# Segment sums moved from the end to the middle of a step, and one block further behind, in a graph network layer

## What is computed

```python
msg_in = jnp.concatenate([node_features[row], node_features[col]], axis=-1)
h = jax.nn.relu(msg_in @ Wm1 + bm1)
h = jax.nn.relu(h @ Wm2 + bm2)
messages = h @ Wm3 + bm3
agg = jax.ops.segment_sum(messages, col, num_segments=num_nodes)
agg = agg / jnp.clip(count, 1.0)[:, None]
```

## Time and profile before

| what | us |
|---|---|
| median of three runs | 1428.48 |
| lowest and highest | 1424.92 and 1430.98 |
| the profiled execution | 1430.17 |
| its span, first to last instruction | 1428.2 |
| PE busy in the span | 1289.8 (90%) |
| DVE busy | 994.0 (70%) |
| ACT busy | 732.5 (51%) |
| POOL busy | 760.7 (53%) |

### The profile page before, as it was taken

The page is one execution under the profiler, slowest core; times in us unless marked ns, Lnnn a source line. Parts: engine busy times, 40 slices in busy tenths (PEclk is TensorE's granted clock), DMA queues, the critical chain, the costliest instruction groups (busy, mean ns, idle before and its releaser), DMA issues.

```text
span 1428.2 us, 32880 instructions
## 1 busy us (share of the span) xinstructions
PE 1289.8 (90%) x9777; PEld 1184.9 (83%) x9778; DVE 994.0 (70%) x2126; ACT 732.5 (51%) x1323; POOL 760.7 (53%) x806
## 2 busy tenths in 40 slices
PE   5887999999999999999999999999888888987997
PEld 4766999999999898998988888888888888884564
DVE  4334777777777777777777777777777777774555
ACT  2433666565655555555555555555555554542322
POOL 4007777666666666666666666666556565610000
PEclk8767999999999999999999999999999999999999
DMA  6866666555555555555555544555455444410001
GB/s 166 287 228 187 180 177 176 167 170 160 172 157 159 161 163 153 156 157 156 153 153 156 150 148 144 152 150 151 137 149 145 141 150 133 150 53 1 20 26 46
DMA packets 152019, 208.50 MB, mean 146 GB/s; under 512 B 23801, under 2 KB 120553, under 8 KB 151978
## 3 DMA queue, kind: packets, MB, share of 16 engines
q1 hardware_dynamic: 113502, 104.44, 24.7%
q0 software_dynamic: 37632, 102.81, 24.1%
q10 hardware_dynamic: 844, 0.79, 0.3%
HBM read 185.15 MB, written 22.80 MB: 146 GB/s over the span
## 4 chain that ended last, share of the span: by engine, by line
PE 74%; DVE 10%; issue 8%; DVEq 3%; ACT 2%; DMA 2%; ACTq 1%; SPq 0%; POOL 0%
PE bank L932 30%; PE bank L911 11%; PE bank L892 8%; PE bank L894 6%; PE bank L879 6%; DVE onehot L670 3%; DVE agg L684 3%; PE bank L845 3%; ACT h L487 2%; PE bank L980 2%; PE bank L993 2%; PE bank L981 1%; PE bank L969 1%; DVE bank L702 1%; PE bank L957 1%
## 5 line engine op out<-in xcount | busy, mean ns | idle before, releaser
L420 POOL DMA_INDIRECT a_edge<-a_table,src_idx x784 | 743.7, 949 | 487.2 <-PE bank L911 263.5
L932 PE MATMUL bank<-w,h 128*128 128x256 f32 x4704 | 622.0, 281 | 0.0
L932 PEld LDWEIGHTS bank<-w,h 128*128 128x128 f32 x4704 | 586.1, 189 | 0.0
L487 ACT ACTIVATE h<-bank 128x512 fp32r<-128x512 f32 x392 | 234.8, 599 | 401.3 <-PE bank L879 401.3
L737 DVE SCALAR_TENSOR_TENSOR h_lo<-bank,h_hi 128x512 fp32r<-128x512 f32 x392 | 270.2, 689 | 126.1 <-ACT h_hi L494 123.0
L725 DVE SCALAR_TENSOR_TENSOR h<-bank,h 128x512 fp32r<-128x512 f32 x392 | 270.7, 691 | 74.2 <-ACT h L487 58.9
L892 PE MATMUL bank<-h_hi,onehot 128*128 128x258 f32 x880 | 237.7, 294 | 66.4 <-DVE onehot L670 66.1
L494 ACT ACTIVATE h_hi<-bank 128x512 fp32r<-128x512 f32 x392 | 235.1, 600 | 120.4 <-PE bank L932 120.0
L911 PE MATMUL bank<-ident,a_edge 128*128 128x128 f32 x1568 | 239.8, 275 | 26.2 <-issue 21.6
L670 DVE SCALAR_TENSOR_TENSOR onehot<-iota,first_node,dst_col 128x256 fp32r<-128x256 int16 x440 | 210.3, 478 | 65.7 <-issue 40.1
L892 PEld LDWEIGHTS bank<-h_hi,onehot 128*128 128x128 f32 x880 | 166.4, 189 | 86.4 <-issue 57.2
(11 more groups left out here) (108 smaller groups left out, 569.5 us busy)
## 6 DMA issues: line engine op xcount, KB each, us to landing
b_win<-b_table SPq DMA_DIRECT2D x392, 128.0 KB
rel<-rel_dram SPq DMA_DIRECT2D x196, 128.0 KB, 3.2
a_edge<-a_table,src_idx POOLq DMA_INDIRECT x784
b_table<-work SPq DMA_DIRECT2D x12, 1024.0 KB, 4.8
a_table<-work SPq DMA_DIRECT2D x12, 512.0 KB, 3.2
f_x<-in_x SPq DMA_DIRECT2D x12, 256.0 KB, 5.4
out<-work SPq DMA_DIRECT2D x12, 256.0 KB, 2.3
work<-in_L_gnn_Wm ACTq DMA_DIRECT2D x2, 256.0 KB, 6.0
```

The source lines that it names most:

```text
L420: pool.indirect_dma_start(a_edge[:, b % R * TB + t, :], None, a_table, bass.IndirectOffsetOnAxis(ap=src_idx[:, b * TB + t:b * TB + t + 1], ...
L487: act.activation(h1[:, k % 2, 0, :], bank[k % 2][:, :], ACT.Relu).then_inc(s_h1h, 1)
L932: ins = pe.matmul(to, h1[:, j, a, h * EB + t * P:h * EB + (t + 1) * P], w2[:, b, h, :], start=False, stop=(a == 1 and h == KH - 1), skip_g ...
```

## The change

On PE the segment sums move: in step k, S(k-3) now stands behind E(k) and ahead of W(k-1), where it was S(k-2) behind W(k-1). At a border S'(k-3) comes behind S(k-3) and no longer ahead of it. The last pass has one more step.

On DVE a step is now OT(k+1), D2(k-2), D1(k), F(k-3), O(k-2), O'(k-2). D2 is done one step later than before, and ahead of D1; F comes behind D1, and ahead of O. Inside F the bank `SUM` is added first, then `SUM_MORE`; an addition no longer waits for the one ahead of it, and the zeroing waits for the addition from `SUM` alone. The test for far one-hots (line 665) moves from ahead of O to behind it. The words for PE and DVE are laid out for the new distance, with one more bit (2^20) for O' of the next step; that is two more small DVE instructions in the setup. ACT, POOL and SP are as before.

```diff
         def steps(i):
-            return range(U + 2) if isinstance(i, int) and i == NI - 1 else range(U)
+            return range(U + 3) if isinstance(i, int) and i == NI - 1 else range(U)
...
             def add_sums(b, w):
-                dve.wait_ge(s_add, added)
                 dve.reg_add(added, added, 1)
...
-                with dve.If(word > 2**14 - 1):
+                with dve.If((word & 64) > 0):
+                    dve.wait_ge(s_sg, i * U + (k + 1))
+                    add_sums(SUM, within(w, 0, NW - 1))
+                dve.reg_mov(summed, added)
+                further = (word >> 14) & 63
+                with dve.If(further > 0):
                     dve.wait_ge(s_sgm, more)
                     add_sums(SUM_MORE, within(w + 1, 1, NW - 1))
...
                 with dve.If((word & 64) > 0):
-                    dve.wait_ge(s_sg, i * U + (k + 1))
-                    add_sums(SUM, within(w, 0, NW - 1))
-                    dve.wait_ge(s_add, added)
+                    dve.wait_ge(s_add, summed)
                     dve.memset(bank[SUM][:, 0:HC], 0.0).then_inc(s_add, 1)
...
+                    if there(i, k) and there(i, k + 1):
+                        if (k + 1) % 2 == 0:
+                            dve.wait_ge(s_rc[(k + 1) // 2 % RC], (i + (k + 1) // U) * 16 + 16)
+                        make_onehot_t(k + 1)
                     if there(i, k - 2):
-                        make_onehot(k % 2, i, k - 2, 0, s_oh)
+                        dve.wait_ge(s_h2h, i * U + (k - 1))
+                        dve.scalar_tensor_tensor(h2_lo[:, k % 2, :, :],
...
+                    if there(i, k - 3):
+                        with dve.If((word & (64 + 63 * 2**14)) > 0):
+                            finish_sums(i, k - 3, word)
                     if there(i, k - 2):
-                        with dve.If(word > 2**14 - 1):
+                        make_onehot(k % 2, i, k - 2, 0, s_oh)
+                        with dve.If(word > 2**20 - 1):
                             make_further_onehot(i, k - 2, 1)
...
+                    if there(i, k - 3):
+                        pe.wait_ge(s_h2l, i * U + (k - 2))
+                        pe.wait_ge(s_oh, i * U + (k - 2))
+                        sum_segments(bank[SUM], (k - 3) % 2, k - 3, False).then_inc(s_sg, 1)
+                        with pe.If(word > 127):
+                            with pe.Fori(1, within(word >> 7, 1, NW - 1) + 1):
+                                sum_further(k - 3)
                     if there(i, k - 1):
                         j = (k - 1) % 2
...
-                    if there(i, k - 2):
-                        pe.wait_ge(s_h2l, i * U + (k - 1))
-                        pe.wait_ge(s_oh, i * U + (k - 1))
-                        with pe.If(word > 127):
-                            with pe.Fori(1, within(word >> 7, 1, NW - 1) + 1):
-                                sum_further(k - 2)
-                        sum_segments(bank[SUM], k % 2, k - 2, False).then_inc(s_sg, 1)
```

More of the change, by code:

```diff
@@ L281, in gnn_layer @@
         PE_TOP = NFE + 128 * (NW - 1)
-        DVE_TOP = (NW - 1) + 64 + 128 * NFE + 2**14 * (NW - 1)
+        DVE_TOP = (NW - 1) + 64 + 128 * NFE + 2**14 * (NW - 1) + 2**20
         full = E // EB
@@ L604, in make_words @@
                 dve.tensor_tensor(words_pe[0:1, 0:NB], words_pe[0:1, 0:NB], far, ALU.add).then_inc(s_wz, 1)
-                dve.scalar_tensor_tensor(words_dve[0:1, 2:2 + NB], row_more[0:1, :], float(2**14),
+                dve.scalar_tensor_tensor(words_dve[0:1, 3:3 + NB], row_more[0:1, :], float(2**14),
+                                         words_dve[0:1, 3:3 + NB], ALU.mult, ALU.add).then_inc(s_wz, 1)
+                dve.tensor_scalar(row_flush[0:1, :], row_more[0:1, :], 1.0, None, ALU.min).then_inc(s_wz, 1)
+                dve.wait_ge(s_wz, 7)
+                dve.scalar_tensor_tensor(words_dve[0:1, 2:2 + NB], row_flush[0:1, :], float(2**20),
                                          words_dve[0:1, 2:2 + NB], ALU.mult, ALU.add).then_inc(s_wz, 1)
-                dve.wait_ge(s_wz, 6)
+                dve.wait_ge(s_wz, 8)
                 dve.scalar_tensor_tensor(words_dve[0:1, 0:NB], row_far[0:1, 1:1 + NB], 128.0,
@@ L646, in _ @@
             added = dve.alloc_register("sums_added_dve")
+            summed = dve.alloc_register("sum_bank_read_dve")
+            dve.reg_mov(summed, 0)
             dve.reg_mov(far_t, 1)
@@ L663, in far_onehots_t @@
             def far_onehots_t(k, word):
-                spans = (word >> 7) & 127
-                with dve.If(spans > 0):
-                    with dve.Fori(1, within(spans, 1, NFE) + 1) as j:
-                        make_far_onehot_t(k, j)
+                with dve.Fori(1, within((word >> 7) & 127, 1, NFE) + 1) as j:
+                    make_far_onehot_t(k, j)
             def make_onehot(slot, i, k, w, done):
@@ L688, in finish_sums @@
                 w = word & 63
-                with dve.If(word > 2**14 - 1):
+                with dve.If((word & 64) > 0):
[4 more added lines that the diff above has]
+                with dve.If(further > 0):
                     dve.wait_ge(s_sgm, more)
                     add_sums(SUM_MORE, within(w + 1, 1, NW - 1))
-                    with dve.If(word > 2**15 - 1):
-                        with dve.Fori(2, within(word >> 14, 2, NW - 1) + 1) as j:
+                    with dve.If(further > 1):
+                        with dve.Fori(2, within(further, 2, NW - 1) + 1) as j:
                             dve.wait_ge(s_add, added)
@@ L727, in body @@
                                                  ).then_inc(s_h1l, 1)
+                    if there(i, k - 3):
+                        with dve.If((word & (64 + 63 * 2**14)) > 0):
+                            finish_sums(i, k - 3, word)
                     if there(i, k - 2):
-                        with dve.If(word > 2**14 - 1):
+                        make_onehot(k % 2, i, k - 2, 0, s_oh)
+                        with dve.If(word > 2**20 - 1):
                             make_further_onehot(i, k - 2, 1)
                     if there(i, k) and there(i, k + 1):
-                        if (k + 1) % 2 == 0:
-                            dve.wait_ge(s_rc[(k + 1) // 2 % RC], (i + (k + 1) // U) * 16 + 16)
-                        make_onehot_t(k + 1)
-                    if there(i, k - 1):
-                        dve.wait_ge(s_h2h, i * U + k)
-                        dve.scalar_tensor_tensor(h2_lo[:, (k - 1) % 2, :, :],
-                                                 bank[2 + (k - 1) % 2][:, :].rearrange("p (t h) -> p t h", t=TB),
-                                                 0.0, h2_hi[:, (k - 1) % 2, :, 0:H].bitcast(F32),
-                                                 ALU.max, ALU.subtract).then_inc(s_h2l, 1)
-                    with dve.If(word > 63):
-                        if there(i, k - 2):
-                            finish_sums(i, k - 2, word)
-                        if there(i, k) and there(i, k + 1):
+                        with dve.If((word & (127 * 2**7)) > 0):
                             far_onehots_t(k + 1, word)
```

7 lines of the change are left out of this document (5 added, 2 removed).

## The result

The changed kernel takes 1598.35 us (median of 4 runs, 1593.16 to 1602.48) where the kernel before takes 1426.7 (4 runs): the ratio is 1.120, 95% interval 1.115 to 1.125. It is 12% slower, where 2% faster was forecast. Four runs of a later group (before_pad4, after_lean_align, before_align, after_compactb) come from a time in which every kernel took some 13% longer, the kernel before too (1619 us), so their times are compared with that one only.

A forecast was written before the change was run, and what follows sets the result against it. PE was taken to set the time, so only its holes could be won. 1430.2 - 46.6 (borders) + 11.5 (passes' ends) + 3 + 2 = 1400.1 us for the profiled execution, 1399 for the median, range 1368 to 1424.

The forecast's parts named there:

- What bounds the kernel: PE sets the time, busy 1009 of 1100 us; only its holes at borders (108 us) and passes' ends (43 us) can be won.
- Plain blocks: Blocks away from borders and passes' ends stay at 2.57 us from W to W, priced at zero change.
- The border: Where windows meet: one wait of 0.70 us remains, cost 1.29 in place of 2.26, gain 46.6 us over 48 borders.
- The upper end of the wait: At a border, S's wait for O with the upper ends of DVE's chain: 1.32 us where 0.70 was taken.
- the lowest gain: All 48 borders with the upper ends of DVE's chain: 48 x 0.35 = 17 us.
- The pass's end: PE's own hole goes, but S waits behind ACT's load: 1.14 us in place of 0.90, a loss of 11.5 us.
- the sum: Whole kernel: 1430.2 - 46.6 + 11.5 + 3 + 2 = 1400.1 us for the profiled execution, taken as 1399 for the median.
- rival 4: DVE's start of a pass gets slow by fetching longer code: decides from 2.2 us, 1438 at 3 us; chance 0.03.
- the slack of O: At a pass's start, the some 1.6 us that DVE was said to have in hand.
- Rival 1: At borders DVE's additions don't get shorter, register work not having been hidden: 1425 to 1432 us, no change; chance 0.11.
- Rival 2: At passes' ends ACT's load does not bind and the hole goes altogether: 1343 us; chance 0.07.
- Rival 3: In every block DVE's chain D2, D1, tests, O outlasts PE's block: slower, 1459 us at 0.15 beyond; chance 0.04.

The follow-up runs named there:

- before_pad4: Kernel before with four waits per block added in never-run code of DVE's loop (430 instructions): 1621 us where the kernel before took 1619.
- after_lean_align: The lean form with ACT's words moved seven places, so its load starts at a multiple of eight: ratio 0.973 to the kernel before at 1619.25 us.
- before_align: Kernel before with ACT's words moved so that its load starts at a multiple of eight: ratio 0.999 (0.995 to 1.002).
- after_compactb: Changed kernel, sum bank zeroed in its addition's branch and the word's outer test dropped (408 instructions): 1603.85 us against 1619.25, ratio 0.986.
- lean form: Changed kernel without DVE loop code these data never run (far one-hots, windows beyond the next), 271 instructions: 1387.84 us, 0.973 of the kernel before.
- complete form with 432 instructions: Changed kernel, nothing left out, sum bank zeroed in the same branch as its addition, ACT's words unmoved: 1401.37 us, 0.983 of the kernel before.

## Why the prediction was wrong

It gave the change 1399 us, with a range up to 1424, and the change took 1598. Step by step:

**What bounds the kernel** held. PE's holes at borders and passes' ends are where the time lies, and the runs that removed them moved the time by about as much as they were counted for.

**Plain blocks** held at 2.57, with the two more tests on DVE hidden.

**The border** held. From the start of S to O were 3.03 us where 3.21 were forecast (0.84 to D1, 0.61, 0.58, 0.48, 0.52 against 0.83, 0.70, 0.60, 0.50, 0.58), O to S took 0.63 and not 0.53, and the border cost 1.17 and not 1.29 (median 1.15). The upper end of the wait adds up to 1.36 and not to the 1.32 that is written, which moves the lowest gain from 17 to 15 us. The prediction has the far test's move in its chain, but does not say that this 0.35 of the gain could be had without the new order of the sums.

**The pass's end** held in all but the term that decided. PE's own hole went, ACT's load took its place, and the block at the pass's start takes 1.19 beyond a plain one (3.76 in the lean form) where 1.14 was forecast. The complete form with 432 instructions measures 1401, close to the 1399 of the sum, but that is in part luck: its borders cost 1.38 (median), 0.23 more than the changed kernel's. My estimate for the changed kernel without the fetch is 1401 - 48 x 0.23 = 1390, inside the range.

**The step that failed** is rival 4, that DVE's start of a pass gets slow by fetching its longer code. It had the mechanism and the place, stood at nothing in the sum, and got 0.03 of chance and a price of 3 us chosen freely. The runs showed that the loop is fetched anew in each pass, that DVE's idle time there is some 3.9 us longer (4.65 against 0.76), and that this costs 197 us against the complete form of 432 and 211 against the lean form, 4.1 to 4.4 for each pass. Rival 4's own working was too kind as well: with 3.9 us it gives 1400 + 48 x (3.9 - 2.2) = 1482, and 1598 was measured. It counted only the slack of O. The first wait that came is that of E for OT (104.1 us in 46 waits), which the prediction had put at none, and behind the hole PE ran at the lower clock, which makes the second block take 4.39. The argument against it, that DVE's hole at a pass's start was no longer than a load and a branch, was no argument: it shows that the old loop fitted, and says nothing of how near it was to the limit. It was near, 367 of about 384 in the compiled code, and the change added 18. The row on the instruction queue (26 packets for 48 passes) showed that the old loop is not fetched in each pass, and so that a fetch in each would be something new. That row and the two lengths were there to read, and neither was in the sum. Where the limit lies stood in no row, so a cost of that size beside gains of 30 us should have made the range reach far above 1424.

The Trainium skill (Runtime: NRT & Kernel Launch, Instruction fetch mechanics) names the mechanism: a taken branch whose target is not in the pages held waits for a fetch. The traces agree with that, 3.85 us between the branch and its target. The same section puts an engine's code memory at 512 instructions, and by that figure every loop of these runs would have fitted; the runs set the limit for DVE's loop between 383 and 385 compiled instructions, so here the measurement decides.

**Rival 1** (the additions don't get shorter) is refuted by 0.58 between them in place of 0.80. **Rival 2** (ACT's load does not bind) is refuted by the edit of its place, which gave 1.19 us a pass. **Rival 3** did not come.

Not settled: why the limit lies near 384, which is three packets of 128 instructions of 64 bytes, and why 4.8 packets come for each pass where a loop of 385 fills little more than three. That the engine also fetches past the loop's end, and keeps room for that, would explain both; no run tests it. No run moves a loop of 361 to 383 instructions, either.

## What to carry to other kernels

Before moving or adding code in a long loop on an engine, count the instructions of the loop's body in the compiled code, with the code in branches that are never taken, and look at the packets of the instruction queue: if they are few and the loop is long, the next few instructions can cost more than any order can win. After taking a wait away, ask what is late next, and test that by its own edit: here a load of words that cost the old order next to nothing (4 us) was worth 4% in the new one.

## What the hardware showed that I had not expected

- The DVE loops of up to 383 compiled instructions were not fetched again, those of 385 and more in every pass (24 to 26 against 256 to 259 packets in all), with a hole of 3.85 us between branch and target in the pass shown, at each of the three places tried. In 48 passes it cost 197 to 211 us in one order, 234 and 257 in the other.
- A load of eight words into ACT's registers took 1.76 us from a place one word behind a multiple of eight (counted from the start of the tile), and 0.55 from a multiple of eight.
- After 2.2 us of idleness PE's granted clock was 0.57 over the next 8 us, and one W took 2.76 in place of 1.58.
- The row of a compare-and-branch at the loop's end (line 258) is 47 to 63 ns long on DVE, where the Trainium skill (Advanced Engine Details and Errata, Control Flow Timing) gives 108 for one. But the row's length is not the price: in the kernel before, the branch of the far test starts at 394.50 and the next row at 394.70 (the second line stands in the earlier trace rows), 0.20 us later. With its two register operations the test was worth 0.35 us for each border, once nothing covered it.

```profile
394.50 0.06 DVEq L665
```
